# Half of a batch's ranking placed behind the first two units of maxima of the next batch, in an eight-batch transformer block

## The reference

```
def _L0_ffn_ref(x, w_router, w_block):
    k = max(1, int(L * CAPACITY_RATIO))
    scores = jnp.einsum('bld,d->bl', x, w_router)
    _, top_idx = jax.lax.top_k(scores, k)
    selected = jnp.take_along_axis(x, top_idx[:, :, None], axis=1)
    processed = jax.nn.gelu(jnp.einsum('bkd,de->bke', selected, w_block))
    out = x.at[batch_idx, top_idx].set(processed)
...
x = x + 0.5 * _L0_ffn_ref(_layernorm(x, axis=-1), L0_ffn_w_router, L0_ffn_w_block)
x = x + _L0_attn_ref(_layernorm(x, axis=-1), L0_attn_Wq, ...)
x = x + 0.5 * _L0_ffn_ref(_layernorm(x, axis=-1), L0_ffn_w_router, L0_ffn_w_block)
```

## Time and profile before

| | us |
|---|---|
| median of 3 runs (2589.05 to 2590.61) | 2589.89 |
| the profiled execution | 2591.08 |
| its span | 2589.4 |
| TensorE busy | 2348.7 (91%) |
| VectorE busy | 1719.9 (66%) |
| ScalarE busy | 1181.7 (46%) |
| GpSimd busy | 395.1 (15%) |

### The profile page before, as it was taken

One profiled execution on the slowest core, in us unless ns is written; L12 is line 12 of the kernel. 1 busy time (PEld: TensorE's weight loads), 2 busy tenths in 40 slices (PEclk: granted clock), 3 DMA queues, 4 the chain that ended last, 5 costly groups with the idle time before them and its releaser, 6 DMA issues.

```text
span 2589.4 us, 53629 instructions
## 1 busy us (share of the span) xinstructions
PE 2348.7 (91%) x21888; PEld 1457.0 (56%) x21888; DVE 1719.9 (66%) x4806; ACT 1181.7 (46%) x2071; POOL 395.1 (15%) x510
## 2 busy tenths in 40 slices
PE   6769999899989998899998999989999899998976
PEld 4534567445664556645575546654476545674445
DVE  4658656785667756686566865678656785567735
ACT  3325543464425643356433554445543455424542
POOL 0101211112101121111111101111111112101121
PEclk9879999999999999999999999999999899999998
DMA  3200021100201002010111101210021100301000
GB/s 122 98 2 2 2 85 47 66 2 8 92 34 66 3 18 82 33 67 2 35 64 50 51 2 66 66 66 3 2 83 49 66 2 2 98 1 67 2 1 33
DMA packets 70034, 106.20 MB, mean 41 GB/s; under 512 B 3104, under 2 KB 33312, under 8 KB 67744
## 3 DMA queue, kind: packets, MB, share of 16 engines
q1 hardware_dynamic: 69792, 102.77, 11.6%
HBM read 64.49 MB, written 37.75 MB: 39 GB/s over the span
## 4 chain that ended last, share of the span: by engine, by line
PE 69%; DVE 12%; issue 10%; ACT 6%; POOL 2%; DMA 0%; DVEq 0%; POOLq 0%; ACTq 0%
PE psum L722 25%; PE psum L735 18%; PE psum L841 9%; PE psum L848 7%; PE psum L738 4%; DVE psum L973 4%; ACT pr L703 4%; PE psum L764 3%; PE psum L749 3%; DVE part L971 2%; DVE junk L923 1%; POOL rstd L596 1%; DVE junk L921 1%; DVE qk L960 1%; DVE nt_l L909 1%
## 5 line engine op out<-in xcount | busy, mean ns | idle before, releaser
L703 ACT ACTIVATE pr<-psum 128x512 f32<-128x512 f32 x1152 | 617.6, 597 | 621.3 <-PE psum L738 621.1
L735 PE MATMUL psum<-qk,qk 32*128 32x512 f32 (+3 forms) x4608 | 511.4, 369 | 97.8 <-ACT pr L703 38.9
L973 DVE CUSTOM_DVE_ANT_0 psum<-psum,mask_b 128x512 f32<-128x512 f32 (+3 forms) x1024 | 473.1, 522 | 166.6 <-PE psum L749 165.1
L735 PEld LDWEIGHTS psum<-qk,qk 32*128 32x128 f32 x4608 | 320.6, 186 | 402.9 <-ACT pr L703 123.0
L749 PE MATMUL psum<-qk,qk 32*128 32x512 f32 (+3 forms) x4608 | 514.1, 373 | 29.1 <-DVE part L971 19.6
L971 DVE TENSOR_REDUCE part<-psum 128x1 f32<-128x512 f32 x512 | 325.2, 681 | 71.7 <-PE psum L749 69.9
L749 PEld LDWEIGHTS psum<-qk,qk 32*128 32x128 f32 x4608 | 312.7, 189 | 57.5 <-DVE part L971 26.1
L614 POOL TENSOR_SCALAR_AFFINE_SELECT pr<-pr 128x512 f32<-128x512 f32 x256 | 158.0, 635 | 1056.6 <-ACT pr L703 1056.6
L841 PE MATMUL psum<-pr,v_sb 128*32 128x512 f32 (+3 forms) x3072 | 312.4, 502 | 1.6 <-ACT acc_sb L622 1.6
L848 PE MATMUL psum<-pr,ones 128*32 128x512 f32 (+3 forms) x3072 | 306.1, 493 | 0.0
L643 ACT ACTIVATE norm<-x,nmr,rstd 128x512 f32<-128x512 f32 x192 | 152.4, 810 | 193.4 <-DVE nmr L903 193.4
(11 more groups left out here) (115 smaller groups left out, 3411.4 us busy)
## 6 DMA issues: line engine op xcount, KB each, us to landing
x<-x_dram SPq DMA_DIRECT2D x16, 1024.0 KB, 6.8
spill_x<-x SPq DMA_DIRECT2D x16, 1024.0 KB, 5.2
x<-spill_x SPq DMA_DIRECT2D x16, 1024.0 KB, 7.7
out_dram<-x SPq DMA_DIRECT2D x16, 1024.0 KB, 5.1
w_h<-scratch_o SPq DMA_DIRECT2D x28, 256.0 KB, 3.1
w_l<-scratch_o SPq DMA_DIRECT2D x28, 256.0 KB, 3.3
w_h<-scratch_q SPq DMA_DIRECT2D x6, 1024.0 KB, 4.9
w_l<-scratch_q SPq DMA_DIRECT2D x6, 1024.0 KB, 6.9
```

The lines of the kernel that those rows point to most:

```text
L703: nc.scalar.activation(pr_of(b, g, u)[:, 2 * p + place, :], bank(e, place), ACT.Exp, scale=SCALE).then_inc(exp_ready, 1)
L735: eng.matmul(o, (k_h, k_h, k_l)[t][own, P * j:P * (j + 1)], (q_h, q_l, q_h)[t][own, queries], start=(t == 0 and at == 0), stop=False, skip ...
L973: m = nc.vector.tensor_tensor_reduce(scores, scores, mask_b[:, BANK - w:BANK], 1.0, FAR, ALU.add, ALU.max, top_of)
```

## The change

The ranking pieces RT 4 to RT 7 of the second feed-forward step leave `back(b)` for all batches but the last: RT 4 and RT 5 now stand behind step 0 of the next batch's first group, RT 6 and RT 7 behind step 1. `ending(b - 1)` is spread from step 2 to step 10 instead of from step 0 to step 8.

```diff
-        out += layer(1, b, 5) + [("RT", 1, b, i) for i in range(2, NT)]
+        out += layer(1, b, 5) + [("RT", 1, b, i) for i in range(2, TC if b + 1 < B else NT)]
...
-            groups[0][0] += [("F", 1, b - 1, 6)]
-            groups[0][1] += [("F", 1, b - 1, 7), ("G", 1, b - 1, 6), ("G", 1, b - 1, 7)]
+
+            groups[0][0] += [("F", 1, b - 1, 6), ("RT", 1, b - 1, 4), ("RT", 1, b - 1, 5)]
+            groups[0][1] += [("F", 1, b - 1, 7), ("G", 1, b - 1, 6), ("G", 1, b - 1, 7), ("RT", 1, b - 1, 6), ("RT", 1, b - 1, 7)]
             tail = ending(b - 1)
...
-            groups[0] = [weave(groups[0], tail, 0, len(groups[0]) // 2)]
+            groups[0] = [weave(groups[0], tail, 2, len(groups[0]) // 2 + 2)]
```

## The result

The changed kernel takes 2567.32 us (median of 4 runs, 2563.9 to 2573.03) against 2590.06 before (median of 4): a ratio of 0.9915, 95% interval 0.9896 to 0.9934. It is faster by 22.7 us, half of the 46.3 us forecast, and above the range given (2535 to 2556). The profiled execution took 2565.99 us with a span of 2564.3, 25.1 less than the span before.

What follows compares the result with a forecast made beforehand. TensorE carries most of the chain but waits for VectorE's ranking at seven batch boundaries. Each gains its window - 5.32 us less lateness, 46.3 us in all: 2589.9 - 46.3 = 2543.6 us, range 2535 to 2556.

Steps and rivals of the forecast that it cites:

- The stall and its removal: Before step 1, TensorE idles 3.83 us at batch 1 for step 0's reduction; moving r4 to r7 removes it.
- VectorE's and ScalarE's model of steps 2 to 4: At batch 1 both engines' limits meet within 0.1 us at steps 3 and 4; step 4 taken at D + 12.12.
- D: Start of VectorE's reduction of step 0's maxima after the change; forecast 457.66 at batch 1.
- The 2.65 us to step 3: At batch 1, time from F7's end through ScalarE's gelu, table load and exponential to step 3, which gave 467.73.
- Rival 2: Stall moves to step 2 or 3: 0.6 to 1.2 us at seven boundaries, 2548 to 2552 us; chance 0.07.
- RF, its GpSimd steps and the combining: Ranking's closing sums, eight GpSimd products and combining, two steps later: charged nothing, without cover 2 us in all.
- the later dip: Lower clock in the thin stretch of steps 2 to 4 (0.84 in batch 1): left as it is, nothing charged.
- rival 1: The clock dip only moves, to the thin stretch at every boundary: 15 us, result 2558 us; chance 0.09.
- The sign that it had named: Prediction wrong if the clock falls in steps 2 to 8; it also named waits for reductions or loads.
- Beside GpSimd's products: Three combining steps instead of one beside the products, 0.04 us each by one row: 0.08 us a boundary.
- Rivals 3 and 4: Late load of x makes it slower, 2595 us; step 1 waits for something else, 2590 us; chance 0.02 each.

Runs made afterwards that it cites:

- e1: Changed kernel with all eight GpSimd products of the old batch's ending right behind RF, ahead of step 9's mask: 2551.41 us, ratio to before 0.9852.
- e3: On top of e1, 6 unread matmuls behind step 2 and 3 behind step 3 at each boundary: 2539.36 us, ratio to before 0.9805.
- e5: Changed kernel plus only 6 unread matmuls behind step 2 and 3 behind step 3, GpSimd's order unchanged: 2556.2 us, ratio to before 0.9875.
- e2: Kernel before with only the ending moved to steps 2 to 10, all ranking pieces left in front of step 0: 2611.6 us, ratio 1.0081.
- e4: On top of e1, the ending spread over steps 1 to 9, RF ahead of the maxima of step 2: 2561.78 us, ratio to before 0.9894.

## Why the prediction was wrong

*The stall and its removal: right.* Step 1 stands behind F6 without idle, and F7 runs at full clock. The forecast's 46.3 us were counted to the start of step 4 on TensorE. There the seven boundaries have 45.2 us (6.04, 6.16, 6.16, 6.03, 6.58, 8.35, 5.84, each counted from the table load, as in the table).

*VectorE's and ScalarE's model of steps 2 to 4: right.* At batch 1 D is 458.98. Maxima 1 came at D + 4.53 (forecast 4.66), maxima 2 at D + 9.06 (9.20), RF took 0.84 (0.93), step 3 began at D + 10.01, released by ScalarE (forecast 10.07 by ScalarE and 9.99 by VectorE), step 4 at D + 12.04 (12.12). Step 3 is at D + 10.01 at all seven boundaries, released by ScalarE in batches 1, 2 and 5 and by VectorE in the others. Step 4 is 0.6 to 0.7 us later than forecast in batches 3, 4 and 7, where step 3's scores already run at a lower clock (the first takes 0.64 to 0.75 us against 0.50). The 2.65 us to step 3 in the prediction are counted from the gelu's start at 471.11, 0.10 behind step 2's start, and not from F7's end: a slip without weight. Rival 2 did not happen.

*The failed step: "RF, its GpSimd steps and the combining".* It said of the two products behind the mask that nobody waits for them before steps 9 and 10, and charged nothing, or 2 us at most. It had the order right and did not follow the wait. The mask of step 9 cannot start before step 9's exponentials, so product 6 comes after them, while combining 6 stands in VectorE's queue for the same step 9 and the maxima of step 10 behind it. The wait passes from ScalarE to GpSimd to VectorE to TensorE, 1.63 us seven times and a dip behind two. e1 puts its price at 16 us. The bank was not "wanted a step later" with time to spare either: the maxima of step 10 begin at 488.22, and step 11 waits for them until 489.33. "Long after all eight could be done" was true and beside the point: GpSimd sat idle 9.97 us with the two products ready behind the mask, since it takes its queue in order.

*The clock: a mis-sized term.* The prediction left the later dip as it was, a term of nothing, and gave rival 1 (15 us) a chance of 9%. What came lies between: 8.8 us are lost from step 2 to step 10, where 46.3 - 38.6 = 7.7 us are missing against the forecast, and e3 shows 12 us to be had by filling 2.1 us of gaps at each boundary. The sign that it had named, a clock that falls in steps 2 to 8, was there at all seven boundaries. That the long idle went away did not protect the thin stretch. In batches 3 and 5 of the kernel before, the clock is 1.00 from step 2 to step 10; there the changed kernel has 0.83 and loses 2.8 and 2.9 us.

*The two together.* From 46.3 forecast the gain went to 38.6 at step 10 (the clock) and to 24.0 at step 16 (the queue and its dips), against 25.1 of the whole span. Without the queue's stall the time is 2551.41 us (e1), inside the stated range; with the stall, and without the dip between steps 2 and 10, it is 2556.2 (e5).

*Beside GpSimd's products.* The prediction took 0.04 us a combining step from one row (0.78 against 0.74). After the change two such steps beside the products took 1.05 and 1.08 at batch 1, and combining 6 took 1.18 beside product 7. The Trainium skill, GPSIMD Engine Reference, section Specifications, has VectorE and GpSimd share SBUF interfaces with contention for instructions with two SBUF inputs; the trace agrees, with 0.3 to 0.5 us for most such steps (0.74 to 1.26 us over the seven boundaries), and the one row I had picked was a mild case (batch 6 of the kernel before has 1.19). Its price by itself was not measured; TensorE's new wait of 1.63 us holds some 0.4 us of it.

*Rivals 3 and 4.* The statistics wait for a load of x once, at the start of the kernel, before as after. Step 1 waited for nothing but the reduction: with it moved, the idle is gone at all seven boundaries.

## What to carry to other kernels

When work moves past another engine's instruction in an in-order queue, ask not whether its input is ready but what the instruction now in front of it waits for, and then follow who is queued behind its own consumer. After removing a stall look at the stretch behind it too: here a stretch of TensorE with short gaps lost the full clock, and a few matmuls that nobody reads, placed in waits that are there anyway, were worth 12 us. Count a gain at several points behind the change, not only at the first: step 2 showed all of it, step 16 half.

## What the runs showed of the hardware

TensorE fell to its lower level in a stretch that was 6.09 us busy of 8.50, with no idle over 1.57 us (granted 0.80 in batch 1). The same stretch had 1.00 with 9 matmuls more. Behind a lone idle of 1.63 us it fell in batches 2 and 5 of the changed kernel and not in the other five; in e2 in batches 3 and 7, in e5 in batches 1, 4 and 5. The time of one kernel scatters with the clock: the changed kernel's four runs lie 9 us apart, the longest (2573.03) at a mean clock of 0.966 and the shortest (2563.9) at 0.969; the first kernel's lie 1.6 apart in that comparison, but 9 in the one of e1 to e4.

A change of ScalarE's table cost 1.28 us and nothing besides: the last gelu ends at 466.92, table load at 466.94, exponential at 468.23. The Trainium skill, ScalarE: Activation LUTs, section What ACT_TABLE_LOAD costs, gives about 1283 ns for the load and about 1380 ns of drain on top, 2.66 us a switch; the first agrees with the trace, the second doesn't show in it.

```profile
466.94 1.28 ACT L704 ACT_TABLE_LOAD   x1
468.23 1.08 ACT L704 ACTIVATE pr<-psum 128x512 f32<-128x512 f32 x2
```
